# A graph-attention layer with a quantised linear layer: another division of the projection stage's side work over the tiles and engines

## The reference

```python
x = x + gnn(layernorm(x), [src, dst], W, att_src, att_dst, bias)
x = x + ffn(layernorm(x), weight, bias)

# gnn: xp = (x @ W) in 4 heads of 256; edges and self loops
a_src = einsum('nhc,hc->nh', xp, att_src); a_dst = einsum('nhc,hc->nh', xp, att_dst)
e     = leaky_relu(a_src[src] + a_dst[dst], 0.2)
ee    = exp(e - segment_max(e, dst)[dst]);  alpha = ee / segment_sum(ee, dst)[dst]
out   = relu(segment_sum(xp[src] * alpha, dst) + bias)

# ffn: rows of x and of weight in blocks of 32: scale = max|block| / 7.5,
# values rounded to the FP6 (E2M3) grid and scaled back, then xd @ wd.T + bias
```

## Time and profile before

| | us |
|---|---|
| median of 3 runs (lowest, highest) | 1623.39 (1621.95, 1625.46) |
| the profiled execution | 1626.81 |
| its span, first to last instruction | 1625.1 |
| `normalise` in the span | 0 to 138.4 |
| `project`, to the end of its matmuls | 138.4 to 606.96 |
| rest | 606.96 to 1625.1 |

### The profile page before, as it was taken

How to read it: one execution, slowest core, us unless ns; L and a number is a source line. 1 busy time by engine, 2 the same in 40 slices (tenths; PEclk the granted TensorE clock), 3 DMA queues, 4 the chain that set the end, 5 groups by cost and what they waited for, 6 DMA issues and landing times. The chain is left out here.

```text
span 1625.1 us, 36740 instructions
## 1 busy us (share of the span) xinstructions
PE 1407.4 (87%) x10949; PEld 973.0 (60%) x10949; DVE 1258.1 (77%) x2681; ACT 855.6 (53%) x2181; POOL 694.3 (43%) x630
## 2 busy tenths in 40 slices
PE   6995578768799995899999999999999269999997
PEld 5883344434444434788888888888888124444443
DVE  7885388977787326778888888888888699999990
ACT  4664011111222536788888888888888234344331
POOL 1003310110101406876667667776666134444441
PEclk9997599988899997999999999999999679999999
DMA  6774183422135527899899989999998446767632
GB/s 218 263 260 147 39 292 115 135 101 102 64 117 175 188 92 251 275 320 319 313 337 320 344 304 338 334 323 331 319 338 308 148 152 168 185 166 172 184 70 44
DMA packets 111796, 352.36 MB, mean 217 GB/s; under 512 B 24610, under 2 KB 24882, under 8 KB 111468
## 3 DMA queue, kind: packets, MB, share of 16 engines
q0 software_dynamic: 69504, 223.72, 41.9%
q1 hardware_dynamic: 38860, 126.82, 22.7%
q10 hardware_dynamic: 3360, 0.91, 0.2%
HBM read 307.66 MB, written 68.88 MB: 232 GB/s over the span
## 5 line engine op out<-in xcount | busy, mean ns | idle before, releaser
L1651 PE MATMUL sum_ps<-xg,wgt 128*128 128x256 f16 x5280 | 601.1, 273 | 57.1 <-DMA xg<-d_xp,tables 27.0
L1623 ACT ACTIVATE wgt<-hot,tables 128x128 f16<-128x128 f16 x1760 | 543.8, 388 | 104.0 <-DVE hot L1562 66.7
L1651 PEld LDWEIGHTS sum_ps<-xg,wgt 128*128 128x128 f16 x5280 | 501.2, 98 | 120.7 <-ACT wgt L1623 44.7
L1538 POOL DMA_INDIRECT xg<-d_xp,tables x432 | 429.4, 994 | 182.7 <-issue 141.5
L1435 PE MATMUL xp_ps<-w,xh 128*128 128x512 f16 x1200 | 295.9, 399 | 36.9 <-DVE w L1038 34.7
L1604 DVE TENSOR_TENSOR acc<-sum_ps,acc 128x1024 f32 x220 | 269.4, 1225 | 0.0
L2020 PE MATMUL fmm_ps<-wdT,tables 128*128 128x512 f16 x1200 | 265.3, 381 | 0.0
L1435 PEld LDWEIGHTS xp_ps<-w,xh 128*128 128x128 f16 x1200 | 116.3, 101 | 171.0 <-issue 33.5
L1366 ACT ACTIVATE xp<-xp_ps,half_scale 128x1024 f16<-128x1024 f32 x25 | 27.8, 1113 | 339.4 <-PE xp_ps L1447 339.4
L2020 PEld LDWEIGHTS fmm_ps<-wdT,tables 128*128 128x128 f16 x1200 | 115.8, 98 | 148.2 <-issue 13.7
L1570 DVE TENSOR_TENSOR wgt<-hot,tables 128x512 f16<-128x512 f16 x440 | 169.8, 435 | 0.1
(11 more groups left out here) (300 smaller groups left out, 1530.1 us busy)
## 6 DMA issues: line engine op xcount, KB each, us to landing
d_xnT<-xnT SPq DMA_DIRECT2D x25, 512.0 KB, 3.0
tables<-d_lo SPq DMA_DIRECT2D x40, 320.0 KB, 3.7
pxnT<-d_xnT SPq DMA_DIRECT2D x25, 512.0 KB, 4.7
d_xp<-xp SPq DMA_DIRECT2D x25, 512.0 KB, 2.7
d_own<-xp_own SPq DMA_DIRECT2D x25, 512.0 KB, 3.9
own_row<-d_own SPq DMA_DIRECT2D x25, 512.0 KB, 4.1
wdT<-in_x_dram SPq DMA_DIRECT2D x24, 512.0 KB, 5.1
xr<-in_x_dram SPq DMA_DIRECT2D x24, 512.0 KB, 5.5
```

What stands on the lines that cost most here:

```text
L1538: nc.gpsimd.indirect_dma_start(out=xg[s][u][:, :, :].rearrange("p a n -> p (a n)"), out_offset=None, in_=d_xp, in_offset=bass.IndirectOffs ...
L1623: last = nc.scalar.activation(wgt[j % WB][u][:, h, :], hot[j % TURN][u][:, :], ACT.Copy, scale=col(numT[:, h, :], u, k))
L1651: last = nc.tensor.matmul(sum_ps[s][:, h * C:(h + 1) * C], w[u][:, a * HEADS + h, :], x[u][:, b, h * C:(h + 1) * C], start=(u == 0 and h % ...
```

## The change

It does five things, all in `project` but for one buffer that moves to the outer function:

- The tiles are taken in the order 24, 0, 1, ..., 23. Tile 24 is the last that `normalise` transposed, and its buffer `xnT0`, now shared by both blocks, still holds it; it isn't loaded.
- In tile 0 of the loop, `w_rest` runs two chunks ahead of TensorE, and there are 4 units, behind every second group. Tile 11 then has 5 units where it had 1.
- The quantised blocks go to tiles 4, 6, ..., 18, one each, and are written two tiles later.
- The one-hots of all 40 batches are made by GpSimd. The 25 scatters stand one by one between them, as do the step ends' gathers and the divisions and multiplications of blocks 0 to 3.
- The small transposes of the edge chain use `gat_ps` instead of `g_ps`.

```diff
-    FIRST_UNITS, NEXT_UNITS, BUSY = 8, 7, 11
+    FIRST_UNITS, NEXT_UNITS, BUSY = 4, 7, 11
+    order = [LAST] + list(range(LAST))
+    quant = {QUANT + 2 * o: o for o in range(KC)}
+    FLAT = 28
+    batch_at = lambda t: (FIRST_UNITS + (t - 1) * NEXT_UNITS) // 2
...
+            def prepare(b):
+                at = b % LB
+                pool.wait_ge(digits_in[at], 16 * (b // LB + 1))
+                if b >= LB:
+                    pool.wait_ge(gat_done, 2 * (b - LB + 1))
+                nc.gpsimd.tensor_scalar(oh[at][:, :], digits[at], lane[:, :], None, ALU.is_equal).then_inc(oh_ready, 1)
...
+            for b in range(2, BATCHES):
+                prepare(b)
+                if b - 2 < TILES:
+                    scatter(b - 2)
...
+                for t in quant:
+                    if t <= BUSY and b == batch_at(t):
+                        divide(quant[t])
+                    if t <= BUSY and b == batch_at(t) + 5:
+                        multiply(quant[t])
             pool.wait_ge(scattered, 16 * TILES)
             nc.gpsimd.dma_start(head[:, :, :].rearrange("p c v -> p (c v)"),
...
-                nc.vector.tensor_scalar(oh[s][:, :], digits[s], lane[:, :], None, ALU.is_equal).then_inc(oh_ready, 1)
...
+            x_rest(0)
+            w_rest(0)
             parts_of_logits()
             prepare(0)
             prepare(1)
-            x_rest(0)
+            w_rest(1)
             for c in range(KC):
-                w_rest(c)
-                unit(units(0)[c])
+                if c + 2 < KC:
+                    w_rest(c + 2)
+                if c % 2:
+                    unit(units(0)[c // 2])
...
             for t in range(BUSY + 1, TILES):
+                o = quant.get(t)
+                if o is not None:
+                    power = divided(o)
...
+                if o is not None:
+                    least = step_of(o, power)
+                    close = near(o, least)
+                    bits = cut(o, close)
+                    rounded(o, bits)
+                if t - 2 in quant:
+                    wd_rest(quant[t - 2])
+                if t + 1 in quant:
+                    inverse(quant[t + 1])
...
-                o = t - QUANT - 1
-                if 0 <= o < KC:
+                if t - 1 in quant:
+                    o = quant[t - 1]
                     pe.wait_ge(wq_ready, o + 1)
```

More of the change, by code:

```diff
@@ L208, in program @@
             w16 = sb("w16", [P, KC, 2, D], F16)
+            xnT = [sb(f"xnT{j}", [P, KC, P]) for j in range(2)]
             low = sb("low", [P, 2])
@@ L276, in normalise @@
         wT = [room[:, (XS + j) * D:(XS + j + 1) * D] for j in range(2)]
-        xnT = [sb(f"xnT{j}", [P, KC, P]) for j in range(2)]
+        xnT = g["xnT"]
         part_max = sb("part_max", [P, KC])
@@ L821, in project @@
         sb, ps, sem = maker(ctx)
-        xnT = [sb(f"pxnT{j}", [P, D]) for j in range(2)]
+        xnT = [a[:, :, :].rearrange("p c n -> p (c n)") for a in g["xnT"]]
         xh = [sb(f"xh{j}", [P, 2, KC, P], F16) for j in range(2)]
@@ L1002, in _ @@
                                 d_head.rearrange("(p c) v -> p (c v)", c=EC)).then_inc(head_in, 16)
[L1004 to L1018, removed]
+            for t in sorted(quant):
+                if t <= BUSY:
+                    continue
+                o = quant[t]
+                divide(o)
+                if t == BUSY + 7:
+                    pool.wait_ge(segmax_out, 16)
+                    highest(range(0, 5))
+                multiply(o)
+            pool.wait_ge(num_out, 16)
+            for c in range(CH):
+                gather(nrow[c], d_num, step_i[:, c:c + 1], rows_in)
+            highest(range(5, TILES))
             pool.wait_ge(tile_out, 32)
@@ L1055, in prepare @@
             def prepare(b):
-                masked[b] = one_hots(b)
+                masked[b] = masks(b)
             def select(u):
@@ L1279, in _ @@
                         x_rest(t + 1)
+                    if s == 2 and t - 2 in quant:
+                        wd_rest(quant[t - 2])
                     if t == 1 and s == 2:
@@ L1332, in _ @@
                     x_rest(t + 1)
-                if 0 <= t - QUANT - 2 < KC:
-                    wd_rest(t - QUANT - 2)
+                if o is not None:
+                    least = step_of(o, power)
[3 more added lines that the diff above has]
+                if t - 2 in quant:
+                    wd_rest(quant[t - 2])
+                if t + 1 in quant:
+                    inverse(quant[t + 1])
                 if t == BUSY + 9:
@@ L1436, in products @@
                                              start=(c == 0 and a == 0 and b == 0), stop=False)
-                    if c < len(todo):
+                    if t == 0 and c % 2:
+                        unit(todo[c // 2])
+                    if t >= 1 and c < len(todo):
                         unit(todo[c])
```

106 lines of the change are left out of this document (60 added, 46 removed).

## The result

| | before, us | changed, us |
|---|---|---|
| median of 7 runs (lowest, highest) | 1622.87 (1621.4, 1626.8) | 1630.57 (1624.35, 1633.79) |
| ratio to before, 95% interval | | 1.0039 [1.002, 1.0058] |
| the profiled execution | 1626.81 | 1628.64 |
| `project`, to the end of its matmuls | 606.96 | 611.12 |
| TensorE, VectorE, GpSimd busy | 1407, 1258, 694 | 1416, 1311, 843 |

The change made the kernel slower by 0.4%, where 1549 us were forecast.

The account below looks back on a forecast made before the run. Bound: a TensorE-VectorE ring in tile 0, VectorE leading tiles 1 to 11, TensorE from 12. Terms -38.5 - 42.7 + 6.9 = -74.3 from 1626.8 give 1552.5, less 3.4 for the median: 1549 us, range 1528 to 1584.

Parts of the forecast that it names:

- GpSimd against VectorE: Tiles 1 to 11: GpSimd's one-hots take 1.3 us a batch (at most 2.4); holding VectorE costs 6 us (0 to 25).
- Rival (a): To tile 11, GpSimd and VectorE exclude each other: 71 half one-hot waits, 46 us less 8 absorbed; 1581 us, chance 0.12.
- It keeps up: GpSimd's one-hots and scatter take 2.6 us a batch (3.7 by the upper price) against a batch period of at least 3.9.
- `oh` as TensorE's main releaser: Sign in the profile after that the forecast is wrong: TensorE mainly waits for the one-hots.
- masks over 0.6 us: Sign in the profile after that GpSimd's SBUF work holds VectorE's masks.
- Theory L: From the experiments: GpSimd's one-hots come too late for TensorE's units, VectorE is not held; unused GpSimd one-hots would cost nothing.
- the ring: Tile 0: TensorE's groups wait for `w_rest`, queued behind units waiting for TensorE; about 7 us a turn, 2.5 of matmuls.
- No wait of 3.5 us in tile 0: Sign expected in the profile after: tile 0 has no wait of that length.
- rival (d): Tile 0 stays in its ring because GpSimd delivers the first one-hots late; 1588 us, chance 0.03.
- Blocks at every second tile: Quantised blocks in alternate tiles: the 5.02 us `wd_rest` stall goes; tiles 6 to 10 take 90.9 us, before 133.4.
- rival (b): VectorE bounds tiles 12 to 18: 14 us instead of 5, and 6 for the low clock; 1564 us, chance 0.11.
- Rival (c): Tiles 0 to 11: GpSimd becomes the bound, slower from 6.3 us a one-hot; at 6.8, 1643 us, chance 0.04.

Follow-up runs that it names:

- e8: e1 plus 40 spare GpSimd TENSOR_SCALARs of 128x640 in several forms, results unused: ratio 0.9585 to the kernel before.
- e10: The changed kernel with each batch's one-hots made by two GpSimd instructions of 640 elements instead of one of 1280: 1571.46 us, 0.9694 of before.
- e9: The changed kernel again, untouched, on another chip: 1629.09 us, 1.0041 of the kernel before.
- e11: Repetition of e1 (changed kernel, one-hots back on VectorE) on the chip of e9 and e10: 1554.60 us, 0.9584 of before.
- e3: e1 plus GpSimd making one-hots of 1280 elements that nobody uses or waits for: ratio 1.0084 to the kernel before.
- e1: The changed kernel with the one-hots back on VectorE, everything else of the change kept: ratio 0.9561 to the kernel before.
- e2: The kernel before with only GpSimd's one-hots, and its scatters, divisions and multiplications between them: ratio 1.0316 to the kernel before.

## Why the prediction was wrong

*The step that failed* is the one called "GpSimd against VectorE", in both of its numbers.

- Its price of one batch's one-hots, 1.3 us "nearer to the first", with 2.4 as the upper bound. Measured 3.54 in the median, 3.61 in the mean. The bounds were not bounds: the MEMSET reads nothing, and the TENSOR_TENSOR of 1.91 us handles 1024 elements, so 2.4 for 1280, but one input is not cheaper than two there: 640 elements take 1.9 to 2.2 us (e8, e10). The estimate of 1.1 us from the Trainium skill's figure (GPSIMD Engine Reference, "Performance versus the Vector engine") fell by the same measurement.
- Its price of the holds, 6 us, 25 "if nearly all meet". Measured: about 67 us in tiles 1 to 11 of the changed kernel; from e9 to e11 the whole time falls by 74 us. Rival (a) had the mechanism: masks, `xh` and quantising steps wait. It priced it at half of 1.3 us for 71 instructions, 46 us less 8 absorbed. With the measured 3.54 its formula gives 71 x 1.77 = 126 us: too much, as most of them miss (the median mask is free). In the changed kernel's tiles 1 to 11, 27 instructions last longer than in e11 (15 of the 36 masks, 2 `xh`, 9 quantising steps, the cast), by 2.4 us each in the mean: 64 us.
- "It keeps up": a batch was to take GpSimd 2.6 us with its scatter, 3.7 at most, against 3.9 of TensorE's. With the measured price it is 3.54 + 1.28 = 4.8 us, and TensorE waited 45 us for one-hots. The sign named for this, `oh` as TensorE's main releaser, came about level with VectorE's answer (45.0 and 45.3 us); the sign of holds, masks over 0.6 us, came true.
- The argument held against rival (a), that GpSimd starts when VectorE is mostly in its product, which reads PSUM, was right of the start and failed by the length. The product is never held (0.66 to 0.68 us in all 79), and GpSimd does start inside one (193.16, in the product from 192.67 to 193.34), but it lasts far longer, and the mask that follows, at 193.26, waits for its end.

*Theory L's share.* TensorE's waits for `oh`, 45 us of the stretch, are real, but e3 is as slow without any wait for GpSimd's one-hots, and e10 is 58 us faster with 32 us of them left. How much of the changed kernel's loss lateness alone would cost isn't measured; the holds account for it within a few us.

*What held.* e11 is the forecast kernel with the one-hots back on VectorE. The forecast without it: 1549 less 6 of holds, plus 36 x 0.46 = 17 for the one-hots where VectorE leads, at most, so 1543 to 1560; measured 1554.6.

- Tile 0: the ring is gone, tile 1 starts at 163.56 in e11 (forecast 162.4 to 174.6, value 167) and at 172.3 in the changed kernel, where `w_rest(1)` still stops TensorE for 3.70 us at 151.71. "No wait of 3.5 us in tile 0" was wrong by that one. It is a hold, too: `w_rest(1)` stands behind the mask of 7.40 us (above). The two one-hots took until 150.3, and TensorE's first unit came at 154.24, behind that second group; so lateness, rival (d)'s reason, isn't what stopped it.
- Blocks at every second tile: `wdT` no longer stops TensorE; tiles 1 to 11 take 215.0 us in e11 against 253.2 (forecast 210.5, with cheaper VectorE units).
- Tiles 12 to 24: 158.0 (cut as e11's are) and 157.8 against a forecast of 155.2. The 5 us for VectorE's long scans were a fair price; rival (b), with 14 and 6 of low clock, would have had 170.
- Rival (c), slower by GpSimd as the bound, was put at 6.3 us a one-hot. The kernel came out slower at 3.54: (c) counted GpSimd's own time alone and left VectorE's holds out.
- The range, 1528 to 1584, left out what rival (a) becomes when the price of an operation that no row shows is outside its "bounds". The chance of slower, 0.04, came from that too. The own forecast's 1529 to 1572 doesn't follow from the terms named for it either, which give 1534 (-4 - 6 - 5) to 1579 (+7 + 14 + 9); the measured time is far outside both.

## What to carry to other kernels

Moving a small operation from VectorE to GpSimd is not free where both work on SBUF: price the move by GpSimd's own time for *that* instruction form (here 6.5 times VectorE's: 3.54 against 0.54 us), then charge VectorE for every two-input or fast-mode instruction that can meet it. If it must be on GpSimd, cut it into shorter pieces: the halves gave back 58 of 74 us here. Count the price in how much longer VectorE's instructions get, not in GpSimd's time: here the stretch followed the former. And where no row shows an operation, a bound from another instruction kind is no bound; the whole forecast hung on it.

The best version measured is e1 (e11): 1554.60 us, 0.9584 [0.9568, 0.96] of before.

## What was not expected of the hardware

- TENSOR_SCALAR on GpSimd at 2.8 ns an element (3.54 us for 1280), 2.9 to 3.4 at 640, whatever the type and operand; MEMSET of 1280 in 1.17 us.
- Holds longer than one GpSimd instruction. A held instruction can go on waiting through the next ones where they follow without a gap: the mask of 7.40 us in the changed kernel lies beside two one-hots, and one of 11.84 us in e2 (452.68 to 464.52) beside three (454.15 to 464.68):

```profile
452.68 11.84 DVE L1077 TENSOR_TENSOR mask<-src_hi,iota_t 128x250 bf16<-128x250 bf16 x1
454.15 10.53 POOL L989 TENSOR_SCALAR oh<-tables,lane 128x1280 bf16<-128x1280 bf16 x3
```

- Having started first doesn't save an instruction: the cast at 185.03 started 0.7 us before the one-hots' recorded start, during a scatter's issue, and ended only with them. Why isn't shown.
- The loss is not in proportion to GpSimd's time: 145 us of long reads cost 90 us (e3), 84 us of half-length ones 4 to 8 (e8), and with 163 us of halves the kernel is 17 us slower than with none (e10 against e11).
